# A four-layer token tower on one core: attentions that project before their buffers are cleared, and a graph whose first twelve edge steps are written out

## The reference

```
L0: embed tokens, neighbours by adjacency and distance | linear attention, 8 heads | 16 experts, 2 chosen
L1: softmax attention, 1 head | graph attention over 262144 edges -> gates of 4 experts
L2: attention over the channels | 8 experts
L3: softmax attention, 8 heads | causal attention with rotated positions | 8 experts

graph attention (L1), 2048 nodes, 4 heads of 4 features:
  h = x @ W;  e = leaky(att_src . h[src] + att_dst . h[dst]) over edges and self loops
  a = softmax of e over the edges of each dst;  out[dst] = sum a * h[src]
  gates = layernorm(out + bias), summed by expert
```

## Time and profile before

| what | us |
|---|---|
| median of three runs | 1116.53 (1110.59, 1116.53, 1117.86) |
| the profiled execution | 1114.76 |
| its span on the core | 1112.5 |
| mean granted TensorE clock | 0.902 of full |

### The profile page before, as it was taken

The page is one execution under the profiler, slowest core; times in us unless marked ns, Lnnn a source line. Parts: engine busy times, 40 slices in busy tenths (PEclk is TensorE's granted clock), DMA queues, the critical chain, the costliest instruction groups (busy, mean ns, idle before and its releaser), DMA issues. The chain is left out here.

```text
span 1112.5 us, 17772 instructions
## 1 busy us (share of the span) xinstructions
PE 946.6 (85%) x6708; PEld 475.5 (43%) x6708; DVE 684.9 (62%) x1757; ACT 393.3 (35%) x697; POOL 166.4 (15%) x179
## 2 busy tenths in 40 slices
PE   2997788989998856884979888999998789889998
PEld 0586566642233234662346442333333334443333
DVE  4977587775555346886566645555552645657665
ACT  1214423245552322221453542444444322353232
POOL 3600032214000022331031000111122102120000
PEclk9979998879997877998898997999999758989999
DMA  9200300000000001000000000000000000000000
GB/s 318 49 1 2 92 1 2 1 1 1 1 1 1 1 1 39 1 0 0 1 1 1 1 1 1 1 1 1 1 1 1 1 1 1 1 1 1 6 6 9
DMA packets 11471, 15.33 MB, mean 14 GB/s; under 512 B 8268, under 2 KB 9324, under 8 KB 10398
## 3 DMA queue, kind: packets, MB, share of 16 engines
q1 hardware_dynamic: 9976, 13.20, 4.0%
q10 hardware_dynamic: 1418, 1.09, 0.4%
HBM read 13.76 MB, written 0.52 MB: 13 GB/s over the span
## 5 line engine op out<-in xcount | busy, mean ns | idle before, releaser
L563 DVE TENSOR_REDUCE mx<-PS 128x2 f32<-128x1024 f32 (+3 forms) x104 | 109.5, 1095 | 105.0 <-PE PS L405 95.6
L525 ACT ACTIVATE arena<-PS 128x1024 f32<-128x1024 f32 (+3 forms) x104 | 91.0, 924 | 138.0 <-PE PS L435 138.0
L1085 DVE TENSOR_TENSOR arena<-arena,PS 128x512 f32<-128x512 f32 (+1 forms) x144 | 95.9, 684 | 60.0 <-ACT arena L1060 55.8
L989 PE MATMUL PS<-XT,late 64*128 64x512 f32 (+1 forms) x288 | 104.4, 665 | 11.0 <-PEq L2204 6.6
L447 PE MATMUL PS<-arena 128*64 128x512 f32 (+3 forms) x416 | 102.1, 581 | 0.5 <-ACT arena L516 0.4
L430 PE MATMUL PS<-arena 32*128 32x512 f32 (+4 forms) x416 | 81.5, 637 | 9.7 <-ACT arena L511 7.4
L1060 ACT ACTIVATE arena<-PS,f_b_sb 128x512 f32<-128x512 f32 x96 | 62.0, 686 | 61.5 <-PE PS L989 60.0
L634 POOL TENSOR_TENSOR H<-H,arena 128x256 f32<-128x256 f32 x36 | 26.1, 726 | 378.2 <-DVE arena L593 375.6
L405 PE MATMUL PS<-arena 32*128 32x512 f32 (+4 forms) x416 | 76.8, 661 | 6.3 <-DVE arena L556 2.8
L1021 PE MATMUL PS<-arena,late 128*64 128x512 f32 (+1 forms) x288 | 79.1, 617 | 0.4 <-DVE arena L1085 0.3
L1770 PE MATMUL PS<-identh 128*128 128x512 bf16 x159 | 55.1, 500 | 24.4 <-PEq L379 11.0
(11 more groups left out here) (406 smaller groups left out, 1670.9 us busy)
## 6 DMA issues: line engine op xcount, KB each, us to landing
arena<-in_rel SPq DMA_DIRECT2D x4, 1024.0 KB, 11.9
late<-in_edges SPq DMA_DIRECT2D x2, 1024.0 KB, 11.2
late<-in_w_f_w SPq DMA_DIRECT2D x3, 342.0 KB
arena<-in_adj SPq DMA_DIRECT2D x1, 1024.0 KB, 6.8
late<-in_w_f_w SPq DMA_DIRECT2D x2, 512.0 KB, 4.2
Cc<-in_consts SPq DMA_DIRECT2D x1, 914.0 KB
arena<-in_ids ACTq DMA_DIRECT2D x1, 800.0 KB
late<-in_w_f_w SPq DMA_DIRECT2D x4, 128.0 KB, 3.9
```

The source lines that it names most:

```text
L525: nc.scalar.activation(PT[:, s % 2, p, :, queries(c)], PS[:, a:a + 2, queries(c)], ACT.Exp, scale=scale).then_inc(exp_done.sem, 1)
L563: v.reduce_max(mx[:, g % 2, c, 2 * p:2 * p + 2], PS[:, a:a + 2, keys(c)], axis=AX.X).then_inc(max_done.sem, 1)
L989: ins = nc.tensor.matmul(PS[0:rows, up_bank(n), :], w1(i)[r], XT2[r, b * S:(b + 1) * S], start=True, stop=True)
L1085: nc.vector.tensor_tensor(HG[0:rows, n % 4, :], ha, PS[0:rows, gate_bank(n), :], ALU.mult).then_inc(gated_done.sem, 1)
```

## The change

- **Attentions.** M3, `minus` and XO are filled by POOL at the head of its queue, in both kinds of attention (linear attention: XO). PE projects at once and waits only ahead of its columns (diagonals in the linear one); DVE keeps VO alone. The four adds of the last group (two pairs) are made by DVE, right behind its own normalising, and POOL's part ends before them.
- **Keys.** A group's `draw` takes the 16 best of its own 256 keys (two rounds of 8) into `drafted` (128 wide), in place of 8 of 2048. During layer 0's experts DVE draws `drawn_keys` out of the 128 drafted ones in 8 rounds (`keys_drawn`, called behind each unit's gated product), and at units 44, 48 and 50 it counts what is still undrawn over all 2176 columns: if anything live is left, the count plus 64 goes to the number of steps.
- **Graph.** During the graph's entry DVE splits the first 48 keys at once and makes the one-hots of steps 0 and 1 (`first_edges`); `graph_nodes` zeroes PSUM by PE and ACT; POOL clears a little more (`graph_zeros`); `graph_start` is gone. `graph_lists` and `graph_sums` stay as loops for what lies beyond 64 and 48 keys, with a new `counted`: one outer test, then two nested loops. The first twelve steps are written out in `graph_end`, with buffers of their own: two or four one-hot buffers deep, and `hatt`, `sm` as before. Two DMAs that copy weights go from `graph_sums` to `graph_end`.
- **Entries.** Numbers of unread matmuls: 5 instead of 4 ahead of and 5 instead of 4 or 2 within the norms where there are two norms with a residual; 3 in place of 2 where there are products and no gates.

The diff, cut to what the text speaks of:

```diff
-                eng.wait_ge(vo_ready.sem, at(vo_ready, 6))
                 for g in range(min(2, G)):
                     proj(g)
...
                 if TB < U:
                     rows(TB)
+                eng.wait_ge(vo_ready.sem, at(vo_ready, 2))
+                eng.wait_ge(xo_ready.sem, at(xo_ready, 3))
...
-                v.memset(M3[:], 0.0).then_inc(vo_ready.sem, 1)
                 v.memset(VO[:], 0.0).then_inc(vo_ready.sem, 1)
-                v.memset(minus[:], -1.0).then_inc(vo_ready.sem, 1)
-                v.tensor_copy(XO[:], values[:]).then_inc(vo_ready.sem, 1)
-                eng.wait_ge(vo_ready.sem, at(vo_ready, 3))
-                v.memset(XO[:, :, D - 1:D], 1.0).then_inc(vo_ready.sem, 1)
+                eng.wait_ge(vo_ready.sem, at(vo_ready, 0))
                 v.tensor_scalar(VO[:, :, D:D + 1].rearrange("p a b -> p (a b)"), C["last"].to_broadcast([P, 4]), ones, None, ALU.mult).then_inc(vo_ready.sem, 1)
                 eng.wait_ge(vo_turned.sem, at(vo_turned, 0))
                 nv = max(NV // 2, 1)
...
+                        else:
+                            eng.wait_ge(xo_ready.sem, at(xo_ready, 0))
...
+                        if g == G - 1:
+                            eng.wait_ge(heads_normed.sem, at(heads_normed, n))
+                            eng.wait_ge(heads_added.sem, at(heads_added, 2 * (G - 1) * NPAIR - 1))
+                            for j in range(2):
+                                if p or j:
+                                    eng.wait_ge(last_added.sem, at(last_added, 2 * p + j - 1))
+                                y = dst[:, batch(g, j) * TB:(batch(g, j) + 1) * TB, :]
+                                v.tensor_tensor(y, y, ON[:, n % 2, j, :].rearrange("p (c d) -> p c d", d=D), ALU.add).then_inc(last_added.sem, 1)
...
+                nc.gpsimd.memset(M3[:], 0.0).then_inc(xo_ready.sem, 1)
+                nc.gpsimd.memset(minus[:], -1.0).then_inc(xo_ready.sem, 1)
+                nc.gpsimd.tensor_copy(XO[:], values[:]).then_inc(xo_ready.sem, 1)
+                eng.wait_ge(xo_ready.sem, at(xo_ready, 2))
+                nc.gpsimd.memset(XO[:, :, D - 1:D], 1.0).then_inc(xo_ready.sem, 1)
...
                         outs(g - 1)
-                outs(G - 1)
-                eng.wait_ge(heads_added.sem, at(heads_added, 2 * G * NPAIR - 1))
...
-            if r:
-                eng.wait_ge(drawn.sem, 2 * r)
-            nc.vector.max(best_of(r), key).then_inc(drawn.sem, 1)
-            eng.wait_ge(drawn.sem, 2 * r + 1)
-            nc.vector.match_replace(key, best_of(r), key, GONE).then_inc(drawn.sem, 1)
+            part_of = key[:, r * EPP // G:(r + 1) * EPP // G]
+            for k in range(2):
+                best_of = drafted[:, 16 * r + 8 * k:16 * r + 8 * k + 8]
+                if r or k:
+                    eng.wait_ge(drafts.sem, 4 * r + 2 * k)
+                nc.vector.max(best_of, part_of).then_inc(drafts.sem, 1)
+                eng.wait_ge(drafts.sem, 4 * r + 2 * k + 1)
+                nc.vector.match_replace(part_of, best_of, part_of, GONE).then_inc(drafts.sem, 1)
...
-                unread(5, 6)
-                eng.wait_ge(vo_ready.sem, at(vo_ready, 4))
                 for g in range(min(2, G)):
                     proj(g)
                 unread(8, 6)
+                eng.wait_ge(vo_ready.sem, at(vo_ready, 2))
+                eng.wait_ge(xo_ready.sem, at(xo_ready, 1))
...
+                nc.gpsimd.tensor_copy(XO[:], values[:]).then_inc(xo_ready.sem, 1)
+                eng.wait_ge(xo_ready.sem, at(xo_ready, 0))
+                nc.gpsimd.memset(XO[:, :, D - 1:D], 1.0).then_inc(xo_ready.sem, 1)
+                for n in range(2 * G - 2):
...
+                        if between is not None:
+                            between(eng, n)
...
+    def keys_drawn(eng, n):
+        v = nc.vector
+        r, k = divmod(n - 8, 4)
+        if 0 <= r < AHEAD and k % 2 == 0:
+            best_of = drawn_keys[:, 8 * r:8 * r + 8]
+            if k == 0:
+                if r:
+                    eng.wait_ge(drawn.sem, 2 * r)
+                v.max(best_of, drafted).then_inc(drawn.sem, 1)
+            else:
+                eng.wait_ge(drawn.sem, 2 * r + 1)
+                v.match_replace(drafted, best_of, drafted, GONE).then_inc(drawn.sem, 1)
+        if n == 44:
+            eng.wait_ge(drawn.sem, 2 * AHEAD)
+            v.tensor_scalar(still, undrawn, -float(2 ** 22), None, ALU.is_gt).then_inc(left_counted.sem, 1)
+        if n == 48:
+            eng.wait_ge(left_counted.sem, 1)
+            v.reduce_sum(peak[:, 5:6], still, axis=AX.X).then_inc(left_counted.sem, 1)
+        if n == 50:
+            eng.wait_ge(left_counted.sem, 2)
+            v.tensor_scalar(peak[:, 6:7], peak[:, 5:6], 0.0, 8.0 * AHEAD, ALU.is_gt, ALU.mult).then_inc(left_counted.sem, 1)
+            eng.wait_ge(left_counted.sem, 3)
+            v.tensor_tensor(peak[:, 5:6], peak[:, 5:6], peak[:, 6:7], ALU.add).then_inc(left_counted.sem, 1)
...
                         nc.tensor.matmul(PS[:, 6, :], identh[:], bc(identh[:], 1, TB), start=True, stop=True, skip_group_check=True)
                 if norms:
-                    dense(4)
+                    dense(5 if len(norms) > 1 and norms[0].plus is not None else 4)
...
                 for k in range(1, ready):
                     eng.wait_ge(norm_steps[0].sem, nv[0] + k)
-                    dense(1 if k == ready - 1 else 4 if long and k <= first[-1] else 2)
+                    dense(5 if long and k < ready - 1 else 3 if products is not None and not gates and len(norms) == 1 and k < ready - 1 else 1 if k == ready - 1 else 2)
...
+        with stage(pe=1, act=1, dve=len(steps)) as (block, tallies):
+            @block.tensor
+            def _(eng):
+                pe, _, _, _ = tallies()
+                nc.tensor.matmul(PS[:, 4, 0:16 * SV], OHd[:, 1, 0, :], spread[:, 0, 0].rearrange("p h v -> p (h v)"), start=True, stop=True, skip_group_check=True).then_inc(pe.up(), 1)
+            @block.scalar
+            def _(eng):
+                _, act, _, _ = tallies()
+                nc.scalar.activation(PS[:, 0:4, 0:16 * (HV + 4)], vals[:, 0, 0, 0:1].unsqueeze(1).to_broadcast([P, 4, 16 * (HV + 4)]), ACT.Copy).then_inc(act.up(), 1)
...
+        with eng.Fori(0, 1) as o:
+            with eng.If(o * span + least < n):
+                many, each = turns
+                with eng.Fori(0, many) as i:
+                    with eng.If(i * (each * span) + base < n):
+                        with eng.Fori(0, each) as k:
+                            with eng.If(i * (each * span) + k * span + base < n):
+                                f(i * each + k)
...
-                counted(eng, n, (8, 8, 4), 8, f, 8 * AHEAD)
+                counted(eng, n, 8 * AHEAD, 8 * AHEAD, (16, 16), 8, f)
...
+        for x in (part(0, [512]), part(512, [2048]), spread.rearrange("p a c h v -> p (a c h v)"), masks[:], vals[:]):
             v.memset(x, 0.0).then_inc(zeros_made.sem, 1)
+        for x in (srclo, srchi, dstlo, dsthi):
+            v.memset(x[:, 0:16], -1.0).then_inc(zeros_made.sem, 1)
         for a, n, k in ((0, HV, 0), (16 * HV, 4, 1)):
             v.tensor_scalar(away[:, a:a + 16 * n].rearrange("p (v h) -> p v h", h=16), bc(C["own"][:, 16 * k:16 * k + 16], 1, n), NEG, None, ALU.mult).then_inc(zeros_made.sem, 1)
-        eng.wait_ge(zeros_made.sem, 6)
...
-    def graph_start():
-        with nc.Block() as block:
-            @block.tensor
-            def _(eng):
-                eng.matmul(PS[:, 4, 0:16 * SV], OHd[:, 1, 0, :], spread[:, 0, 0].rearrange("p h v -> p (h v)"),
...
-            @block.vector
-            def _(eng):
-                split_keys(eng, nc.vector, 0, 0)
...
-                eng.memset(sm[0], 0.0).then_inc(g_vector.sem, LAG * VS)
-            @block.scalar
...
-                eng.memset(sm[1], 0.0).then_inc(g_pool.sem, LAG * LS)
+        v.memset(sm_rest[:, 0:1], 0.0).then_inc(g_vector.sem, LAG * VS)
+        v.memset(sm_rest[:, 1:2], 0.0).then_inc(g_tensor.sem, LAG * PS_)
+        v.memset(sm_rest[:, 2:3], 0.0).then_inc(g_scalar.sem, LAG * AS)
+        v.memset(sm_rest[:, 3:4], 0.0).then_inc(g_pool.sem, LAG * LS)
+        eng.wait_ge(zeros_made.sem, 11)
+    FIRST_KEYS = 48
+    STEPS = FIRST_KEYS // C4
...
+    def step_hots(v, t):
+        at = slice(t * C4, (t + 1) * C4)
+        iota, hi = bc(C["iota"], 1, C4), bc(C["hi"], 1, C4)
+        v.tensor_tensor(sOHs[:, t % 2], iota, bc(skeys[:, 0, at], 2, P), ALU.is_equal)
+        v.tensor_tensor(sOHd[:, t % 4], iota, bc(skeys[:, 2, at], 2, P), ALU.is_equal)
+        v.tensor_tensor(smasks[:, t % 4, :, 0], hi, bc(skeys[:, 1, at], 2, 16), ALU.is_equal)
+        v.tensor_tensor(smasks[:, t % 4, :, 1], hi, bc(skeys[:, 3, at], 2, 16), ALU.is_equal).then_inc(hots_made.sem, 1)
+    def first_edges(eng):
+        v = nc.vector
+        v.tensor_scalar(swhole, drawn_keys[:, 0:FIRST_KEYS], -1.0, None, ALU.mult).then_inc(split.sem, 1)
+        eng.wait_ge(split.sem, 1)
```

(56 more changed lines are left out.)

263 lines of the change are left out of this document (150 added, 113 removed).

## The result

The changed kernel takes **1079.12 us** (median of four: 1072.0, 1074.52, 1083.73, 1095.71) against 1115.47 us of the kernel before (four runs, 1110.59 to 1117.86). The ratio is 0.9658, 95% interval 0.9578 to 0.9739: 3.4% faster. The forecast was 1082 in a range of 1071 to 1096. The profiled execution took 1074.52, with a span of 1072.7 and a mean granted clock of 0.921 (before 0.902).

A forecast was written before the change was run, and what follows sets the result against it. PE was taken to bound most stages, DVE to lead in the edge loop. Graph -21.4, linear attention -2.0, keys +1.7, layer 1 -7, layer 3 -1.9 and -2.0 sum to -32.6: 1114.76 to 1082 us, range 1071 to 1096.

The forecast's parts named there:

- (1): Graph, lists' block: one of eleven tests is left, so DVE's idle of 3.98 us becomes about 2.3.
- (3): Graph, skipped loop block: costs one test too, 2.3 us by the same estimate, ready at 425.2.
- rival 4: Far jump: the skipped loop block jumps over the whole four-step body, 3.4 us more at most, 1085; chance 0.04.
- (4): Graph, first gathered values: turn, copy and gather of one step take 5.3 us, first maximum at 430.5.
- (5): Graph, first to last maximum: 11 periods of 5.6 us, less 0.9 and 0.4, make 60.3, to 490.8.
- (6): Graph, last maximum to gates: 15.2 us less 1.1, to 504.9; 1.0 given back for one slower step.
- Rival 1: Graph's steps: at 1.2 GHz PE sets the step, 6.54 us instead of 5.60, total 1093; chance 0.15.
- (2): Graph: graph_start's 2.9 us go; 4.5 of DVE work moves under 4.8 of idle in the entry, cost nothing.
- Rival 2: Attentions: early starts don't pay, PE's time returns behind, their 11 us are lost, total 1093; chance 0.10.
- Attentions: Linear attention -2.0, layer 1's entry and attention -7, layer 3's two attentions -1.9 and -2.0 us.
- Layer 1's term: Layer 1's entry and attention, -7 us: turns -2.2 if filling keeps the clock, wait 1.64, projection -2.6, last adds -0.6.
- Keys: Layer 0's experts, +1.7 us: draws hidden, count passes of 1.3 and 2.4 cost +0.3 and +1.4 beyond slack.

The follow-up runs named there:

- g_only: Kernel before with the graph part alone, its attentions, draws and unread matmuls kept: 1092.38 us, ratio 0.9823.
- m_body1: Changed kernel with a remainder-loop body of one step instead of four (never executed with this data): 1079.18 us, executed once.
- u_attn: Changed kernel with both attentions as in the kernel before: 1091.85 us, ratio 0.9816 to the kernel before.
- a_only: Kernel before with the changed attentions alone; draws, unread matmuls and graph as before: 1099.97 us, ratio 0.9892.
- u_dense: Changed kernel with the numbers of unread matmuls of the kernel before: 1083.43 us, ratio 0.9734 to the kernel before.
- u_keys: Changed kernel with the draws of before, nothing drawn or counted in layer 0's experts: 1083.92 us, ratio 0.9749 to the kernel before.
- v_count: Changed kernel with the count of undrawn keys cut in four pieces: 1088.26 us, ratio 0.9761 to the kernel before.
- v_both: Changed kernel with the count in four pieces and the further draws put into the remainder loop's block: 1076.34 us, ratio 0.9683 to the kernel before.
- after_again: The changed kernel timed and profiled again without an edit: 1076.54 us, ratio 0.9668 to the kernel before.

## Why the prediction was right, and where not

**Graph, forecast -21.4, measured -22.9 (g_only alone -22.7).** The sum is right by terms that missed in both directions:
- (1) and (3), the two empty blocks. Forecast 2.3 each from the tables to the first turn; measured 409.76 to 416.94 (PE's first turn), 7.2. The step that failed is (3), "the skipped loop block costs one test too". It was rival 4, the far jump, with its price of 3.4 from the exits of the earlier trace rows: the branch took 3.42. The price agrees by luck, though: the exits held eleven tests (six at the outer level, four at the middle, one at the inner), not seven, which at 0.6 each are 6.6 of the 7.61, and no branch there took over 0.24. The rule named there (the Trainium skill, "Runtime: NRT & Kernel Launch", section "Instruction fetch mechanics") agrees with m_body1; no row shows the fetch itself.
- (4), 5.3 to the first values: measured 6.7, with a granted clock of 0.50 from the first turn to the first maximum.
- (5), "11 periods ... I take 5.6": the period is 5.16, and first to last maximum took 55.8, not 60.3. The gap lies in DVE's spaces: from the last score to the one-hots 0.09 (before 465.27 - 465.04 = 0.23), from one-hots to weighting 1.47 (before 1.69), from weighting to maximum 0.14 (before 0.20). In the loop every one-hot raises a semaphore and the waits compare with counts worked out from the turn's number; that this is the cause was argued, no run separates it.
- (6), 14.1 from last maximum to gates: measured 14.25, and the 1.0 for a slow step wasn't needed. Rival 1 is out: none of the steps behind the first is slow.
- (2), the split and one-hots in the entry: 4.3 of DVE work from 393.49, and the projections' copies wait 0.19 behind it. Hidden, as said.

**Slow steps.** The prediction's "in that stretch the granted clock is 0.57" holds for one of the two steps only. Windows of before, the step with the split and the one behind it:

```profile
466.96:474.04 7.08, 4.96 (x46) 3.83 (x47) 6.35 (x22) 1.46 (x4) 2.34 (x1) 1.00 0.00 0
474.04:480.58 6.54, 6.54 (x46) 5.00 (x47) 5.24 (x14) 2.74 (x5) 2.34 (x1) 0.74 0.00 0
```

The 7.08 are at full clock, PE busy 4.96 of them; then the clock falls and PE is busy all 6.54. The same pair stands in the turn before it (7.07, 6.56); behind the third split, at 498.86, no slow step follows. In the changed loop there is no split, and no slow step; that the one brings the other is argued, not shown.

**Attentions, forecast -12.9 together.** The starts came as forecast (forecast in brackets): -1.2 (-1.2), -1.6 (-1.5), -2.2 (-1.6), and -2.0 in layer 1 (-1.6), as 20.64 of u_attn against 18.70 shows. Ahead of the linear attention's projection PE hadn't stood idle, as the prediction has it for every attention: five unread matmuls, 1.25 us up to 116.69, filled the wait, and these went. Of the 0.8 that the linear attention was to gain behind its start, 0.1 is seen where lengths are comparable (g_only 105.2, the changed kernel 105.1), and of the 0.4 of tail in layer 3's attention 0.1. Rival 2 is out. a_only gained 13 as a whole. Layer 1's term, -7, measured -9.5 in the profile, but its step "if the filling keeps the clock, -2.2" is wrong: u_dense has the full-speed turns without the filling, and g_only has them with neither filling nor early start. The kernel before had the clock down there in both profiles, a_only halfway (5.14), the eleven others up. What decides stays open. So 4.8 of this term (2.2 for the turns, 2.6 for the projection) came out right by luck: the clock was up, but not for the reason given. What the early start gives in itself is 2.0; the new attention took 40.9 to 41.0 in nine of the ten profiles that have it and 42.0 in u_keys, the old one showed 40.1, 42.8, 46.0 and 46.0.

**Keys, forecast +1.7, measured +1.8** in layer 0's experts against before, and +2.4 against u_keys, which has the same attentions: 1.9 of it by the two long passes that it named (1.29 and 2.41, forecast 1.3 and 2.4), 0.5 by the draws, which were to be hidden. The draws' gain in the linear attention was 0.3 against u_keys (forecast 0.5).

**What was missing: the clock's part.** 4.5 of the profile's 39.8 us are the linear attention's, which the same code shows at either length. The code effects that the stages show apart from it (-1.2, +1.8, -2.0, -22.9, -1.6, -2.2) sum to -28; the other 8 of the -36.4 between the medians go, as far as the profiles show, with where the half-clock stretches lie. That no run separates: both kernels that were profiled twice repeated their lengths from layer 0 through the graph within 0.5, so part of it may belong to the change after all. The forecast's -32.6 holds 4.8 of clock for a wrong reason and nothing for the rest; that its total came within 3 us of the median is partly luck; between the two profiled executions, which it was summed for, the change is -40.2.

## What to carry to other kernels

A loop that doesn't run can still cost as much as a step that does: look for a long compare-and-branch on PE's sequencer, and keep a body that is usually jumped over short, or out of the path. Cover an added pass on DVE in pieces no longer than the slack per unit. And where TensorE is the bound and its clock moves, judge an edit by the length of its own stage in two profiles; u_keys and v_count saved 2 us in layer 0's experts and took 4 to 5 us more in layer 1's, and v_both, with the same saving, only 1.2.

## What the runs showed that was not expected

The granted clock isn't settled by the code that runs up to a stage: code identical from the start gave 105.2 or 110.1 us in the linear attention and 3.71 or 5.98 in layer 1's turns. Two kernels with 2 us less in layer 0's experts (u_keys, v_count) have medians 7 and 12 us above that of after_again (ratios 0.9749 and 0.9761 against 0.9668, intervals just overlapping), and in their profiles the difference lies in stages that nobody touched. A forward branch over PE's body of four steps took 3.42 us, over one step 0.37 us.
